# Scaling, transposing and multiplying the first groups of the dense stage during the last block of a graph kernel

## What is computed

```python
ZU = einsum('nd,kdr->knr', Z, U)                       # 4 heads of 16
logits = (ZU[:, src] * ZU[:, dst]).sum(-1) / scale
alpha = softmax of logits over the edges of each target node
agg = segment_sum(alpha[..., None] * ZU[:, src], dst)  # numerator / (denominator + 1e-16)
ssa = einsum('k,knr,kdr->nd', softmax(head_w), agg, U)
Z_half = 0.5 * Z + 0.5 * ssa
L0 = relu(Z_half + ETA * ((Z_half - (Z_half @ Dmat.T) @ Dmat) @ Dmat) - ETA * LAM)
x = layernorm(x + L0)
x = layernorm(x + L1(x, src, dst))                     # gathers rows of x by src and by dst
```

## Time and profile before

| what | us |
|---|---|
| median of 3 executions | 2479.98 (2479.67 to 2481.39) |
| the profiled execution | 2478.89 |
| its span, from the first to the last instruction | 2476.7 |

### The profile page before, as it was taken

One profiled execution on the slowest core, in us unless ns is written; L12 is line 12 of the kernel. 1 busy time (PEld: TensorE's weight loads), 2 busy tenths in 40 slices (PEclk: granted clock), 3 DMA queues, 4 the chain that ended last, 5 costly groups with the idle time before them and its releaser, 6 DMA issues.

```text
span 2476.7 us, 61813 instructions
## 1 busy us (share of the span) xinstructions
PE 1835.3 (74%) x15251; PEld 1434.1 (58%) x15252; DVE 1912.4 (77%) x5864; ACT 1157.1 (47%) x3040; POOL 1742.5 (70%) x1832
## 2 busy tenths in 40 slices
PE   9576777767777777677777677777776776896885
PEld 9355555555555556555555555555555555556775
DVE  6676877868778788687777787778777787894888
ACT  2124453544534435444354453444534444466887
POOL 2777777777777777777777777777777773556772
PEclk9555555655555565555655555555565555898997
DMA  9223323233233333333233232332333323894553
GB/s 305 65 54 71 76 61 73 64 67 75 62 70 66 71 72 64 69 67 69 62 73 70 64 72 65 70 69 63 73 69 66 69 63 101 287 332 131 164 164 112
DMA packets 406593, 232.96 MB, mean 94 GB/s; under 512 B 284096, under 2 KB 371434, under 8 KB 406506
## 3 DMA queue, kind: packets, MB, share of 16 engines
q1 hardware_dynamic: 346666, 154.11, 22.6%
q0 software_dynamic: 59840, 77.87, 14.6%
HBM read 134.80 MB, written 42.55 MB: 72 GB/s over the span
## 4 chain that ended last, share of the span: by engine, by line
POOL 34%; issue 23%; DMA 14%; PE 11%; SPq 9%; ACT 3%; DVE 3%; POOLq 2%; ACTq 0%; DVEq 0%
POOL arena L582 34%; DMA arena<-z_table,sslot 14%; SPq L437 8%; PE bank L1508 2%; PE bank L1478 2%; PE bank L1250 2%; POOLq L579 2%; ACT arena L1667 2%; PE bank L1482 1%; ACT L1700 1%; PE bank L1498 1%; PE bank L1510 1%; PE bank L1272 1%; SPq L431 0%; PE bank L1456 0%
## 5 line engine op out<-in xcount | busy, mean ns | idle before, releaser
L582 POOL DMA_INDIRECT arena<-z_table,sslot x1563 | 1508.0, 965 | 529.0 <-issue 447.5
L1353 PE MATMUL bank<-arena 128*128 x4992 | 558.8, 220 | 124.7 <-DVE xin L908 82.7
L1590 ACT ACTIVATE arena<-bank 128x272 f32<-128x272 f32 x416 | 274.6, 661 | 769.9 <-PE bank L1370 756.6
L1353 PEld LDWEIGHTS bank<-arena 128*128 128x128 bf16 x4992 | 444.6, 104 | 248.4 <-issue 146.8
L908 DVE TENSOR_TENSOR xin<-arena,bank 128x512 f32<-128x512 f32 x208 | 143.0, 688 | 393.5 <-DMA arena<-arena 256.6
L1567 ACT ACTIVATE acc<-xTb 128x68 f32 x1600 | 361.1, 311 | 9.2 <-ACT acc L1567 0.5
L1370 PE MATMUL bank<-arena 128*128 128x68 bf16 x1664 | 294.1, 245 | 78.2 <-DVE xto L1042 77.8
L1341 PE MATMUL bank<-ident_b,arena 128*128 128x128 bf16 x1664 | 214.8, 310 | 132.1 <-DVE arena L899 118.5
L1370 PE MATMUL bank<-xto,arena 128*128 128x68 bf16 x3328 | 309.7, 248 | 0.0
L899 DVE TENSOR_SCALAR arena<-iota_b,didx 128x128 bf16<-128x128 bf16 x1664 | 300.8, 275 | 6.5
L1370 PEld LDWEIGHTS bank<-xto,arena 128*128 128x128 bf16 x3328 | 281.5, 133 | 0.0
(11 more groups left out here) (264 smaller groups left out, 2539.6 us busy)
## 6 DMA issues: line engine op xcount, KB each, us to landing
arena<-arena SPq DMA_DIRECT2D x1660, 32.0 KB
arena<-z_table,sslot POOLq DMA_INDIRECT x1563
dspace<-in_xT SPq DMA_DIRECT2D x49, 256.0 KB
xmz_table<-agn SPq DMA_DIRECT2D x49, 256.0 KB
xmz_table<-arena SPq DMA_DIRECT2D x14, 896.0 KB, 8.9
arena<-in_x SPq DMA_DIRECT2D x13, 896.0 KB, 11.2
out<-arena SPq DMA_DIRECT2D x12, 896.0 KB, 4.7
xin<-in_xT SPq DMA_DIRECT2D x8, 896.0 KB, 8.3
```

Source lines behind the costliest of these rows:

```text
L582: pool.indirect_dma_start(ring[:, e % RING, :], None, z_table, bass.IndirectOffsetOnAxis(ap=sslot[:, e:e + 1], axis=0)).then_inc(tiles_in[ ...
L1353: last = T.matmul(zd_ps[g % 2][:, u * KR:(u + 1) * KR], onehotT[:, g * G + u, :], z3[:, bass.ds(tiles[u], 1), s, :].rearrange("p a c -> p ...
L1590: A.activation(sums[:, :, 1 + q * Q:1 + (q + 1) * Q].rearrange("p c j -> p j c"), sum_ps[q % 2][:, 0:Q * AW].rearrange("p (j c) -> p j c", ...
```

## The change

- DVE computes the first part of `rec` (groups 0 and 1) before it begins the last scan, when the states of block `NB - 3` are stored, and the second part (groups 2 to 13) in the loop of the dense stage, ahead of tile 3.
- POOL scales groups 0 and 1 right after it has stored the states of block `NB - 2`, ahead of its share of the last block's states.
- PE no longer waits for the last scan before the dense stage: after the last block's sums it transposes group 0, into banks 4 and 5 instead of 0 and 1, which the scan and the sums use, and computes tiles 0 to 3. Then come 32 products of ones, the wait for `scan_done`, and the transposes of group 1, which stood between tiles 1 and 2. The 64, 16 and 16 products of ones before are gone.
- ACT copies the transposed group 0 ahead of its share of the last block's states, and waits for the other engines' shares before group 1.

SP's program is not touched. The diff, with the moved helper functions cut:

```diff
@@ POOL @@
+            def scale_sums(g):
+                a = acc[:, g * T7:(g + 1) * T7, 0:KR].rearrange("p t (k r) -> p t k r", r=R)
+                nc.gpsimd.tensor_tensor(a, a, spread(rec[...], 3, R), ALU.mult).then_inc(agn_ready, 1)
+
+            pool.wait_ge(rec_ready, 1)
+            for g in range(2):
+                scale_sums(g)
             tiles = last_tiles(mybir.EngineType.Pool, 3)
             pool.wait_ge(scan_done, NB)
...
-            for g in range(NG7):
-                pool.wait_ge(rec_ready, 1 if g < 2 else 2)
...
+            for g in range(2, NG7):
+                pool.wait_ge(rec_ready, 2)
+                scale_sums(g)
@@ DVE @@
             tiles = [last_tiles(mybir.EngineType.DVE, lane) for lane in (1, 2)]
+
+            def reciprocals(t0, t1):
+                V.tensor_scalar(rec[:, t0:t1, :], acc[:, t0:t1, KR:AW], 1e-16, None, ALU.add).then_inc(v_step, 1)
+                dve.wait_ge(v_step, vn.next())
+                V.reciprocal(rec[:, t0:t1, :], rec[:, t0:t1, :]).then_inc(rec_ready, 1)
+
+            dve.wait_ge(xmz_out, 16 * NY)
+            dve.wait_ge(state_stored, B * (NB - 2))
+            reciprocals(0, 2 * T7)
             begin_scan(NB - 1)
...
-            dve.wait_ge(xmz_out, 16 * NY)
-            for t0, t1 in ((0, 2 * T7), (2 * T7, NT)):
...
             for k in range(NT + 6):
+                if k == YB - 1:
+                    reciprocals(2 * T7, NT)
@@ PE @@
+                banks = psum[4:6] if g == 0 else psum[0:2]
                 for t in range(T7):
-                    last = T.transpose(psum[t // 4][...], acc[:, g * T7 + t, 0:KR], ident[:, :])
+                    last = T.transpose(banks[t // 4][...], acc[:, g * T7 + t, 0:KR], ident[:, :])
...
-            pe.wait_ge(scan_done, NB)
-            keep_busy(WARM)
-            pe.wait_ge(rec_ready, 1)
-            keep_busy(WARM // 4)
             transpose_sums(0)
-            keep_busy(WARM // 4)
             for n in range(NT):
...
-                if t % 4 == 0:
+                if n == 0:
+                    pe.wait_ge(aT_ready, 2)
+                elif t % 4 == 0:
                     pe.wait_ge(aT_ready, 2 * g + t // 4 + 1)
...
-                if t == (1 if g == 0 else 0) and g < NG7 - 1:
+                if n == YB - 1:
+                    keep_busy(WARM // 2)
+                    pe.wait_ge(scan_done, NB)
+                    transpose_sums(1)
+                elif t == 0 and 1 <= g < NG7 - 1:
                     transpose_sums(g + 1)
@@ ACT @@
+            copy_sums_T(0)
             tiles = last_tiles(mybir.EngineType.Activation, 0)
...
-            copy_sums_T(0)
+            act.wait_ge(last_stored[1], STORES)
+            act.wait_ge(last_stored[2], 2 * STORES)
             copy_sums_T(1)
```

More of the change, by code:

```diff
@@ L598, in _ @@
                                           ).then_inc(state_stored, 1)
+            def scale_sums(g):
+                a = acc[:, g * T7:(g + 1) * T7, 0:KR].rearrange("p t (k r) -> p t k r", r=R)
+                nc.gpsimd.tensor_tensor(a, a, spread(rec[:, g * T7:(g + 1) * T7, :].rearrange("p t (k a) -> p t k a", a=1), 3, R),
+                                        ALU.mult).then_inc(agn_ready, 1)
+            pool.wait_ge(rec_ready, 1)
+            for g in range(2):
+                scale_sums(g)
             tiles = last_tiles(mybir.EngineType.Pool, 3)
@@ L607, in _ @@
                                       ).then_inc(last_stored[1], 1)
-            for g in range(NG7):
-                pool.wait_ge(rec_ready, 1 if g < 2 else 2)
-                a = acc[:, g * T7:(g + 1) * T7, 0:KR].rearrange("p t (k r) -> p t k r", r=R)
-                nc.gpsimd.tensor_tensor(a, a, spread(rec[:, g * T7:(g + 1) * T7, :].rearrange("p t (k a) -> p t k a", a=1), 3, R),
-                                        ALU.mult).then_inc(agn_ready, 1)
+            for g in range(2, NG7):
+                pool.wait_ge(rec_ready, 2)
+                scale_sums(g)
             def fetch_dst(n):
@@ L1091, in _ @@
             dve.wait_ge(last_stored[2], 2 * STORES)
-            dve.wait_ge(xmz_out, 16 * NY)
-            for t0, t1 in ((0, 2 * T7), (2 * T7, NT)):
-                V.tensor_scalar(rec[:, t0:t1, :], acc[:, t0:t1, KR:AW], 1e-16, None, ALU.add).then_inc(v_step, 1)
-                dve.wait_ge(v_step, vn.next())
-                V.reciprocal(rec[:, t0:t1, :], rec[:, t0:t1, :]).then_inc(rec_ready, 1)
             def inverse_variance(h, m, ready):
@@ L1454, in transpose_sums @@
                 T.nop(nofuse=True)
+                banks = psum[4:6] if g == 0 else psum[0:2]
                 for t in range(T7):
-                    last = T.transpose(psum[t // 4][0:KR, (t % 4) * P:(t % 4 + 1) * P], acc[:, g * T7 + t, 0:KR], ident[:, :])
+                    last = T.transpose(banks[t // 4][0:KR, (t % 4) * P:(t % 4 + 1) * P], acc[:, g * T7 + t, 0:KR], ident[:, :])
                     if t in (3, T7 - 1):
                         last.then_inc(aT_ps, 1)
-            pe.wait_ge(scan_done, NB)
-            keep_busy(WARM)
-            pe.wait_ge(rec_ready, 1)
-            keep_busy(WARM // 4)
             transpose_sums(0)
-            keep_busy(WARM // 4)
             for n in range(NT):
@@ L1639, in _, with copy_sums_T @@
             period(NB - 1, 1, more=False, dense=False)
+            def copy_sums_T(g):
+                if g >= 2:
+                    act.wait_ge(y_ps, (g - 1) * T7)
+                banks = psum[4:6] if g == 0 else psum[0:2]
+                for q in range(2):
+                    act.wait_ge(aT_ps, 2 * g + q + 1)
+                    n = 4 if q == 0 else T7 - 4
+                    A.activation(aT[g % 2][:, q * 4 * P:(q * 4 + n) * P], banks[q][0:KR, 0:n * P], ACT.Copy).then_inc(aT_ready, 1)
+            copy_sums_T(0)
             tiles = last_tiles(mybir.EngineType.Activation, 0)
```

## The result

The change takes 2493.69 us (median of 13 executions, 2482.86 to 2504.81) against 2477.07 for the kernel before (13, 2473.13 to 2481.39): a ratio of 1.0071, 95% interval 1.0056 to 1.0086. It is **slower by 0.7%**; forecast was no difference that can be told (2481.1). The profiled execution took 2497.92 us, with a span of 2496.1.

The account below looks back on a forecast made before the run. PE was taken to set the dense stage's pace, with group 4's late load consuming its lead. Remaining lead -0.94 plus half-clock cost 2.0 gave +1.1 us, 2480.0 for the profiled execution and 2481.1 as median, range 2477 to 2483.5.

Parts of the forecast that it names:

- The first reciprocals: DVE ahead of the last scan: delay of the scan between 0 and 0.77 us, taken as 0.
- The second reciprocals: DVE's dense loop after three tiles: end by 2131.6, covered by 0.7 us before tile 7's product; uncovered, at most 3.0.
- PE's lead: Start of PE's dense stage: tile 7 starts at 2132.3 instead of 2137.51, 5.2 us earlier.
- The term for the start: PE's first dense tiles: 4 us at half clock after the idle stretch lose 2.0 us.
- Where the lead goes: Tile 28's identity product: PE stands 4.2 us for group 4's load, leaving 0.94 us of the lead.
- the sum: Whole kernel: -0.94 of remaining lead plus 2.0 for the stall's half clock, +1.1 us.
- The first rival, a stall without the fall: Tile 28: the stall stays near 2.1 us, the clock stays full, only -0.94 remains, 2479.0 us; chance 0.21.
- What the stall costs: Behind tile 28's stall: PE's clock falls to half, losing between 0 and 2.3 us, taken as 2.0.
- the late load repeats: First tiles of groups 5 to 7: PE stalls and its clock falls each time, +5.1 us or more, 2485.1; chance 0.05.
- The whole lead lasts: Tile 28: group 4's rows land 4 us earlier, so the gain is 5.2 us, 2474.8; chance 0.08.

Follow-up runs that it names:

- run 8: run 6's kernel plus 48 products of ones before the first transposes: 2476.47 us, 1.0006 of before; with second reciprocals also split: 2479.31 us, 1.0037.
- run 1: The changed kernel executed once more, unaltered, for a second profile: 2504.2 us.
- run 6: The change with SP issuing the loads of group 4 and later groups earlier: 2476.26 us, 0.9993 of the kernel before.
- run 4: The kernel before with only group 4's load held back, until 23 instead of 7 tiles are added: 2484.6 us, 1.0040 of before.
- run 5: The kernel before without its 64, 16 and 16 products of ones ahead of the dense stage: 2485.72 us, 1.0038 of before.
- run 2: The change with 64 products of ones ahead of PE's wait for group 4's rows: 2480.41 us, 1.0018 of the kernel before.
- run 3: The change with 64 products of ones right after tile 28, behind the stall: 2485.05 us, 1.0038 of the kernel before.
- run 9: One execution each, comparing the untouched blocks: the kernel before twice more, 2471.78 and 2477.68 us, and run 2's kernel once more, 2478.85 us.

## Why the prediction was wrong

*The first reciprocals*: 0 was taken, 0.8 came, the upper end of the bound; the register loads fill the gap until 0.1 us ahead of them. It delayed the scan and cost nothing further on, as the step said of its other end.

*The second reciprocals*: forecast to end at 2131.6, which is S + 16.9, they ended at 2132.07, S + 16.0, and no wait of PE for DVE shows there in the change. They were covered by 2.5 us, not 0.7; with an earlier tile 7 (run 8) PE waits for DVE.

*PE's lead*: 5.2 forecast, 4.3 and (runs 1 and 6) some 2.8 measured. The term for the start was too small: half clock lasted some 9 us, from 2121 to 2130, not 4, and ended 2.6 us after the ones had begun (0.82 in 2130 to 2131, 1.00 behind).

*Where the lead goes*: right in its place, its cause and its amount: SP's load at S + 34.7 (2150.80), the identity product of tile 28 waits for it, 0.91 of lead left (forecast 0.94); the stall is 3.3 us, not 4.2, since the lead was smaller. One reading on the way was not right: the issue that takes 0.39 does not stand for engines that keep up, for they were full then as well (1.10 and 348 GB/s); no term of the sum rests on it. The first rival, a stall without the fall, does not hold: in run 1 PE stood for 1.7 us and the clock fell, though an idle stretch of 2.1 had left it full in the earlier trace rows. That row was a narrow base: the next stretch of that length in the same trace, from 2310.43, was followed by half clock (0.50 from 2313.8 to 2317.1, last section).

***What the stall costs*** is the step that failed. It took 2.0 us, from 4 us at half clock, with 2.3 or more by rows 7 as the upper end; it measured 19.6 in the profiled execution and 25.4 (54.6 x 0.466) in run 1. The mechanism, a fall of the clock in the stall, was right; the time until it rises was taken from rows with other work behind the idle stretch: products of ones in the earlier trace rows, the second layer in the earlier trace rows, whose clock was indeed back after some 5 us (last section). The dense stage never ran at half clock in the kernel before, so no row of it showed how long its products take to raise it, and the step should have said that this end is unknown and reached far. The runs show it: the same products stay at half clock for 16 to 55 us in the change and in runs 1, 4 and 5, and for 3.4 and 6.8 us in run 8; 64 ones in the stall keep the clock full (run 2), and behind it they end the half clock in under 5 us (run 3). With 19.6 in place of 2.0, the sum is +18.7, and 2479.98 + 18.7 = 2498.7 is within the executions measured (2483 to 2505), whose scatter fits that of the half-clock stretch. The sum has nothing for the blocks. In the two profiles compared they are equal (1964.1 and 1963.8 by the marks of run 9), so the 18.7 holds none of it; in the medians, 16.6 us apart, some 4 us may be theirs, with the cause open.

The rival *the late load repeats* had the sign right and the mechanism wrong: one stall was enough, and groups 5 to 7 did not wait. Its sentence from the Trainium skill, "TensorE: Matmul & The Clock Gate", section "HAM oscillation", that a wait for a load starts the work behind it at half clock, agrees with the profiled execution for that one load: the clock was at 0.50 when PE's work came back at 2159.86. *The whole lead lasts* was right about what the lead is worth: run 6, where the load is early, has it whole at the end of the stage.

## What to carry to other kernels

Work moved forward is worth no more than the next load's margin; read that margin from the landing time and the first use, and move the load with the work (run 6). A stall of 2 or 3 us on PE, when PE sets the pace, is priced by the clock's way back, not by its length: look for a row that shows the same instructions at half clock until the clock rises, and where there is none, keep the range open upward. Cheap products of ones belong into the stall, not behind it (runs 2 and 3).

## What was not expected of the hardware

TensorE's granted clock stayed at 0.50 with PE busy almost throughout: 42 and 55 us (the change), 16 us (run 4), 20 us (run 5), but only 3.4 and 6.8 us in run 8, all f32 products of 64 or 128 rows by 256 columns and transposes. With bf16 products of ones, back to back, it rose 2.6 us after the first of them in the change (2127.78 to about 2130.4) and 3.6 us after in run 3 (2160.27 to about 2163.9); in run 1 the 32 ones began at 2128.53, and it rose 4.7 us later, 1.1 us behind the last of them. At full clock the same f32 products held it for the rest of the stage. And f32 alone is not what delays it: in the kernel before, the second layer's work behind the stretch of the earlier trace rows, f32 as well, has its clock back after some 5 us, and after a shorter stretch, of 2.1 us from 2310.43, it falls and is back after 3.4 us, as the windows there show:

```profile
2281.00:2286.00 5.00, 4.57 (x15) 4.02 (x16) 4.86 (x10) 3.53 (x9) 3.78 (x5) 0.50 0.85 280
2286.00:2291.00 5.00, 5.00 (x35) 4.63 (x35) 1.96 (x13) 2.46 (x6) 3.78 (x5) 0.96 0.37 116
...
2313.80:2317.10 3.30, 3.30 (x14) 2.91 (x15) 3.20 (x9) 1.74 (x5) 2.38 (x4) 0.50 0.94 309
2317.20:2320.00 2.80, 2.80 (x21) 2.63 (x21) 1.84 (x12) 1.76 (x4) 2.19 (x3) 1.00 0.35 102
```

What in the dense products delays the rise, and why by such differing times, no run here separates.
